# Routed rows of a mixture-of-experts layer scattered to their tokens by job, and read back by four plain loads

## The reference

```python
base_y = _silu_mul_mlp(xt, base_gate_up, base_down)      # 256 -> 2*704 -> 256
top_w, top_e = jax.lax.top_k(rw, 2)                      # of 8 experts
combine = (one_hot(top_e, 8) * top_w[..., None]).sum(1)
moe_y = einsum('eth,te->th', expert_outputs, combine)
return moe_y + base_y
```

## Time and profile before

| | us |
|---|---|
| runs | 904.8, 913.33, 916.46 |
| median of the runs | 913.33 |
| the profiled execution, its own time | 920.24 |
| its span | 918.5 |
| PE busy in the span | 830.7 (90%) |
| DVE busy | 518.9 (56%) |
| ACT busy | 415.4 (45%) |
| POOL busy | 343.8 (37%) |

### The profile page before, as it was taken

The page is one execution under the profiler, slowest core; times in us unless marked ns, Lnnn a source line. Parts: engine busy times, 40 slices in busy tenths (PEclk is TensorE's granted clock), DMA queues, the critical chain, the costliest instruction groups (busy, mean ns, idle before and its releaser), DMA issues.

```text
span 918.5 us, 16141 instructions
## 1 busy us (share of the span) xinstructions
PE 830.7 (90%) x5468; PEld 601.0 (65%) x5469; DVE 518.9 (56%) x1277; ACT 415.4 (45%) x907; POOL 343.8 (37%) x654
## 2 busy tenths in 40 slices
PE   4779799999999999999999896866999999999993
PEld 3344486686776876866866775753566666666672
DVE  3666448768888887888888873564511111111114
ACT  2658756556665656656666362113212222222220
POOL 1146358358367465654672581003330000000005
PEclk9889879779989899799799796896999999999997
DMA  7613242141140141031211211009554100110104
GB/s 187 149 30 86 47 123 56 24 103 25 24 127 13 29 111 22 27 104 25 39 38 25 52 41 29 2 24 376 208 205 164 35 31 26 34 33 24 34 23 132
DMA packets 107618, 66.30 MB, mean 72 GB/s; under 512 B 65120, under 2 KB 98976, under 8 KB 107552
## 3 DMA queue, kind: packets, MB, share of 16 engines
q1 hardware_dynamic: 100160, 59.52, 24.0%
q0 software_dynamic: 1536, 4.20, 1.5%
q10 hardware_dynamic: 5856, 1.73, 0.8%
HBM read 50.84 MB, written 14.58 MB: 71 GB/s over the span
## 4 chain that ended last, share of the span: by engine, by line
PE 67%; ACT 4%; POOL 3%; DVE 3%; DMA 3%; issue 2%; SPq 0%; ACTq 0%; DVEq 0%
PE bank L1693 12%; PE bank L637 8%; PE bank L1772 7%; PE bank L683 5%; PE bank L1710 4%; PE bank L794 3%; PE bank L745 3%; PE bank L760 3%; PE bank L721 2%; PE bank L719 2%; PE bank L759 2%; PE bank L1732 2%; PE bank L645 2%; PE bank L764 2%; PE bank L1763 2%
## 5 line engine op out<-in xcount | busy, mean ns | idle before, releaser
L1133 DVE SCALAR_TENSOR_TENSOR y<-bank,cwh,y 128x510 f32<-128x510 f32 (+2 forms) x240 | 177.1, 743 | 48.5 <-ACT y L887 44.4
L637 PE MATMUL bank<-xnT,wbuf 128*128 128x512 f32 x320 | 159.0, 621 | 6.2 <-DVE y L1133 6.2
L1693 PE MATMUL bank<-f_wgu,f_xgT 128*128 x368 | 118.7, 466 | 0.0
L1441 POOL TENSOR_TENSOR term<-inv,blk 128x126 f32<-128x126 f32 (+22 forms) x248 | 87.4, 352 | 47.1 <-DMA blk<-a_blocks 28.3
L2147 POOL DMA_INDIRECT f_back<-slots_y,f_slot x16 | 15.4, 960 | 222.1 <-DMA slots_y<-f_yb 217.0
L1444 POOL TENSOR_TENSOR inv<-inv,term 128x126 f32<-128x126 f32 (+22 forms) x248 | 91.1, 367 | 19.4
L637 PEld LDWEIGHTS bank<-xnT,wbuf 128*128 128x128 f32 x320 | 56.5, 195 | 63.2 <-issue 50.7
L1693 PEld LDWEIGHTS bank<-f_wgu,f_xgT 128*128 128x128 f32 x368 | 66.3, 190 | 37.2 <-issue 7.7
L2049 DVE TENSOR_TENSOR f_act<-f_sg,bank 128x352 f32<-128x352 f32 x46 | 24.0, 521 | 109.5 <-PE bank L1693 109.5
L1857 ACT ACTIVATE f_sg<-bank 128x352 f32<-128x352 f32 x46 | 21.3, 463 | 123.9 <-PE bank L1693 123.9
L887 ACT ACTIVATE y<-bank,cwh 128x512 f32<-128x512 f32 x80 | 54.9, 686 | 36.1 <-PE bank L637 33.8
(11 more groups left out here) (222 smaller groups left out, 1570.5 us busy)
## 6 DMA issues: line engine op xcount, KB each, us to landing
f_wgu<-in_exp_gu SPq DMA_DIRECT2D x8, 1408.0 KB, 9.3
f_wdn<-in_exp_dn SPq DMA_DIRECT2D x8, 640.0 KB, 10.5
dr<-sums SPq DMA_DIRECT2D x16, 256.0 KB, 4.5
ex<-sums SPq DMA_DIRECT2D x16, 256.0 KB, 4.4
blk<-a_blocks SPq DMA_DIRECT2D x32, 128.0 KB, 2.7
slots_x<-oT SPq DMA_DIRECT2D x24, 128.0 KB, 1.9
f_xg<-slots_x SPq DMA_DIRECT2D x24, 128.0 KB, 2.0
slots_y<-f_yb SPq DMA_DIRECT2D x23, 128.0 KB, 1.7
```

Of the source, the lines that this page charges most:

```text
L637: last = mm(bankA[p % 2][:, :], wbuf[A.par][:, kt, wblk, :], xnT[:, kt, (p % 2) * 512:(p % 2 + 1) * 512], start=kt == 0, stop=kt == 1)
L1133: v.scalar_tensor_tensor(out=y[p % 2][:, :, k:], in0=src[:, :, 0:SEQ - k], scalar=cwh[A.par][:, cb, 3 - k:4 - k], in1=y[p % 2][:, :, k:], ...
L1441: g.tensor_tensor(step_term, inv[:, 0:r, j:j + 1].to_broadcast([P, r, k]), blk[:, j:j + 1, j + 1:].to_broadcast([P, r, k]), ALU.mult).then ...
L1693: last = mm(gu[c][:, 0:FFH], xgT[par][:, k, :], wgu[:, e, k, at:at + FFH], start=k == 0, stop=k == 1)
```

## The change

Two DRAM tensors are new. `rows_back` has a row for each choice and token (2 x 1,024 rows of 1 KB, in the order choice, tile, token) and 256 spare rows. `homes` has one 4-byte number for each of the 3,072 slots: the row of `rows_back` that belongs to the slot.

- DVE makes two small integer tables from new columns of the constant masks (`homes`, behind `place`): `home` (16 columns, the row number of each token and choice) and `spare` (24 columns, a spare row for each slot). The masks grow by 40 columns.
- SP writes `spare` over all of `homes` before it waits for the scatter of the rows. Partition p holds the numbers of slots p, 128 + p, 256 + p and so on, so each is an element of 4 bytes by itself.
- POOL, behind the scatter of the rows, scatters `home` into `homes` by 16 indirect DMAs of 128 numbers, through the same `slot` addresses.
- SP waits for these behind `fetch(3)`, and loads `homes` into the SBUF tile `target` (128 x 24 numbers) by one DMA.
- For each job POOL scatters `yb` straight to its rows of `rows_back` through `target[:, m]`, waits until that has landed, and frees the buffer (`f_free`). The 23 plain stores of SP and `slots_y` are no longer used.
- At the end SP waits for the last two scatters and loads `rows_back` by four plain DMAs of 512 KB into SBUF that held the weights of ways 1 and 2. Each covers four tiles and one choice.
- DVE adds in four batches of four. The four adds of a batch touch different tiles and have no wait between them. `add_base` of tile 6 now stands before all batches, that of tile 7 between the second and the third.

```diff
+    back = wgu[:, 1:3, :, :]... [:, 0:2 * TT_N * HID] ...  # (p, choice j, tile n, d)
@@ sync_program
             if e == WAYS - 3:
                 sp.wait_ge(f_x2t, 8)
+                sp.wait_ge(f_homes, 2)
+                sp.dma_start(homes_of.rearrange("(m p) a -> p (m a)", p=P), spare[:, :], ...).then_inc(f_homes, 16)
                 sp.wait_ge(f_scattered, 32 * TT_N)
...
         fetch(3, 1, 1)
+        sp.wait_ge(homes_out, 16 * 2 * TT_N)
+        sp.dma_start(target[:, :], homes_of.rearrange("(m p) a -> p (m a)", p=P), ...).then_inc(f_homes, 16)
         with sp.Fori(0, JOBS // 2 - 1) as i:
-            store(2 * i, 0)
             fetch(2 * i + 4, 0, i + 2)
-            store(2 * i + 1, 1)
             fetch(2 * i + 5, 1, i + 2)
-        for m in range(JOBS // 2 * 2 - 2, JOBS):
-            store(m, m % 2)
+        sp.wait_ge(y_out[0], 16 * ((JOBS + 1) // 2))
+        sp.wait_ge(y_out[1], 16 * (JOBS // 2))
+        for g in range(2):
+            for j in range(2):
+                n0 = j * TT_N + g * TT_N // 2
+                sp.dma_start(back[:, j, g * TT_N // 2:(g + 1) * TT_N // 2, :],
+                             rows_back[n0 * P:(n0 + TT_N // 2) * P].rearrange("(n p) d -> p n d", p=P)).then_inc(back_in[2 * g + j], 16)
@@ vector_program
-            dve.wait_ge(y_out[par], 16 * use + 1)
+            dve.wait_ge(f_free, m + 1)
             v.tensor_copy(yb[par][:, :], dn[par][:, 0:HID]).then_inc(f_y, 1)
...
+        def add_back(g, j):
+            dve.wait_ge(back_in[2 * g + j], 16)
+            if j:
+                dve.wait_ge(f_back, TT_N * g + 4)
+            for n in range(4 * g, 4 * g + 4):
+                v.scalar_tensor_tensor(out=acc[:, n, :], in0=back[:, j, n, :], scalar=small[:, 2 + j, n:n + 1], in1=acc[:, n, :],
+                                       op0=ALU.mult, op1=ALU.add).then_inc(f_back, 1)
@@ gpsimd_program
-        for k in range(2 * TT_N):
-            if k >= 4:
-                pool.wait_ge(f_back, k - 3)
-            g.indirect_dma_start(out=back[k % 4][:, :], out_offset=None, in_=rows_y,
-                                 in_offset=bass.IndirectOffsetOnAxis(ap=slot[:, k % 2, k // 2:k // 2 + 1], axis=0)).then_inc(back_in[k % 4], 16)
+        pool.wait_ge(f_homes, 2 + 16)
+        for n in range(TT_N):
+            for j in range(2):
+                g.indirect_dma_start(out=homes_of, out_offset=bass.IndirectOffsetOnAxis(ap=slot[:, j, n:n + 1], axis=0),
+                                     in_=home[:, j * TT_N + n:j * TT_N + n + 1], in_offset=None).then_inc(homes_out, 16)
+        pool.sem_inc(f_free, 2)
+        pool.wait_ge(f_homes, 2 + 16 + 16)
+        for m in range(JOBS):
+            pool.wait_ge(f_y, m + 1)
+            g.indirect_dma_start(out=rows_back, out_offset=bass.IndirectOffsetOnAxis(ap=target[:, m:m + 1], axis=0),
+                                 in_=yb[m % 2][:, :], in_offset=None).then_inc(y_out[m % 2], 16)
+            pool.wait_ge(y_out[m % 2], 16 * (m // 2 + 1))
+            pool.sem_inc(f_free, 1)
```

More of the change, by code:

```diff
@@ L62, in mask_table @@
     out["filled"] = np.broadcast_to(P * np.arange(TT_N), (P, TT_N))
+    out["home"] = P * np.arange(2 * TT_N)[None, :] + t
+    out["spare"] = 2 * T + P * (np.arange(SLOT_TILES) % 2)[None, :] + t
     return {k: v.astype(np.float32) for k, v in out.items()}
@@ L1504, in feed_forward @@
     dn = t["banks"][6:8]
+    rows_back = nc.dram_tensor("rows_back", (2 * T + 2 * P, HID), F32, kind="Internal").ap()
+    homes_of = nc.dram_tensor("homes", (SLOT_TILES * P, 1), mybir.dt.uint32, kind="Internal").ap()
     masks, gam, gwT = t["masks"], t["gam"], t["gwT"]
@@ L1534, in feed_forward @@
     yb = [sb(f"f_yb{i}", [P, HID]) for i in range(2)]
-    back = [sb(f"f_back{i}", [P, HID]) for i in range(4)]
+    home = sb("f_home", [P, 2 * TT_N], mybir.dt.uint32)
+    spare = sb("f_spare", [P, SLOT_TILES], mybir.dt.uint32)
+    target = sb("f_target", [P, SLOT_TILES], mybir.dt.uint32)
     x2T = sb("f_x2T", [P, KT_H, T])
@@ L1613, in sync_program @@
                 sp.wait_ge(f_x2t, 8)
+                sp.wait_ge(f_homes, 2)
+                sp.dma_start(homes_of.rearrange("(m p) a -> p (m a)", p=P), spare[:, :], allow_slow_non_contiguous=True).then_inc(f_homes, 16)
                 sp.wait_ge(f_scattered, 32 * TT_N)
@@ L2074, in keep_routed, with homes @@
             dve.sem_inc(f_add, 1)
-        def add_back(k):
-            n, j = k // 2, k % 2
-            dve.wait_ge(back_in[k % 4], 16 * (k // 4 + 1))
-            if some(k):
-                dve.wait_ge(f_back, k)
-            v.scalar_tensor_tensor(out=acc[:, n, :], in0=back[k % 4][:, :], scalar=small[:, 2 + j, n:n + 1], in1=acc[:, n, :],
-                                   op0=ALU.mult, op1=ALU.add).then_inc(f_back, 1)
+        def add_back(g, j):
[5 more added lines that the diff above has]
+                                       op0=ALU.mult, op1=ALU.add).then_inc(f_back, 1)
+        def homes():
+            v.tensor_copy(home[:, :], masks[:, MASK_AT["home"][0]:MASK_AT["home"][0] + 2 * TT_N]).then_inc(f_homes, 1)
+            v.tensor_copy(spare[:, :], masks[:, MASK_AT["spare"][0]:MASK_AT["spare"][0] + SLOT_TILES]).then_inc(f_homes, 1)
         dve.sem_inc(f_act, 2 * LEAD)
@@ L2092, in vector_program @@
         place()
+        homes()
         for b in range(3, FT):
@@ L2115, in vector_program @@
         dve.wait_ge(f_add, JOBS + BASE_FIRST)
[L2116 to L2117 removed]
         add_base(JOBS + BASE_FIRST, BASE_FIRST)
[L2119 to L2120 removed]
+        add_back(0, 0)
+        add_back(0, 1)
         add_base(JOBS + BASE_FIRST + 1, BASE_FIRST + 1)
         dve.wait_ge(f_add, TT_N + JOBS)
[L2123 to L2124 removed]
+        add_back(1, 0)
+        add_back(1, 1)
     def gpsimd_program(pool):
```

23 lines of the change are left out of this document (6 added, 17 removed).

## The result

The changed kernel took 929.8 us (median of 4 runs, 924.37 to 933.01) against 913.4 for the kernel before (4 runs, 904.8 to 916.46): ratio 1.018, 95% interval 1.0137 to 1.0224. The forecast was 905.7, in a range of 897 to 914, so it was wrong. The profiled execution took 924.37 us with a span of 922.6, the fastest of its runs, while the one of before (920.24) was slower than all four of its own. So I compare stretches of the spans, not their totals.

What follows compares the result with a forecast made beforehand. PE was taken to bound the jobs, POOL's gathers the end. The end saves 7.6 us, all else hidden or nothing: profiled 920.24 becomes 912.6, and the same step from the median 913.33 gives 905.7 us, range 897 to 914.

Steps and rivals of the forecast that it cites:

- The end: From the last job's copy to span end: four plain loads replace gathers, DVE's adds bound it; 7.6 us less.
- the step's middle estimate: Four end loads of 512 KB: first lands 3.6 us after issue, at 897.9, the others at 900.1, 902.3 and 904.5.
- the gathers' 22 us: POOL's gathers and transfers at the end hold 22.2 us; PE's base work hidden behind them becomes bare, saving only 7.6.
- Sixteen number scatters on POOL: Before job 0, 676.6 to 696.8, sharing DMA engines with the last weights; 0 to 2.4 us on PE's path, taken as 0.
- Both bounds: Price of a 4-byte number packet: 8.9 ns from 4-byte reads, 46 ns from a 1 KB row of an indirect scatter.
- fetch 2 late, PE waits at the turning for job 2: Before job 2: rows land at 694.7, PE turns them at 697.5, so 2.8 us to spare against number scatters.
- The prediction's own sign of being wrong: In the changed profile: number scatters making the last weights land more than 3 us later would show the forecast wrong.
- dear 4-byte writes: Rival, 677 to 700: number writes delay fetch 2; gain shrinks to 5.2 us or becomes a loss; chance 9%.
- Its law: Same rival's mechanism: at c ns a number packet, fetch 2 is late by 112c - 2.8 us and PE waits.
- the step's upper bound: First write of spare numbers: 1.7 to 8.8 us plus 2.0 to land, in by 660.5 to 667.6; hidden.
- SP's wait for the numbers: Ahead of fetch 4: numbers in by about 698.3, SP at fetch 3 only at 700.55, so no wait.
- Casts, masks, POOL's scatter in the loop, jobs of 8.59 us: Casts 0.4 us, hidden; masks 0.1 us, taken as nothing; POOL's scatter about 3 us of each 8.59 us job, taken as nothing.

Runs made afterwards that it cites:

- e3: Changed kernel without any number traffic through DRAM, job places from a fixed table; median 906.3 us, ratio 0.9897 to the kernel before.
- e2: Changed kernel without the 16 number scatters, first write of spare numbers kept, places from a fixed table; 908.6 us in its one execution.
- v1b: v1 run again, unchanged, on the chip that showed late releases in e4b and e5; median 931.3 us, ratio 1.0196 to the kernel before.
- e1: Changed kernel with the first write of spare numbers in runs of 96 bytes instead of single numbers; median 934.2 us, ratio 1.0211.
- s1: Changed kernel with POOL waiting for the adds of the first six tiles before the number scatters; median 921.2 us, ratio 1.0054.
- e5: Changed kernel without a number table: number and expert ride in each routed row, POOL works out targets per job; median 907.8 us, ratio 0.9916.
- e4: Changed kernel with the numbers 512 bytes apart in DRAM, first execution; 907.6 us, stretch 232.90.
- v1: e3 plus the 16 number scatters in their old place before job 0, with nothing waiting for them; median 933.9 us, ratio 1.0169.
- v5: v1 with each number scatter waiting until the one before has landed; median 931.9 us, ratio 1.0153 to the kernel before.
- s3: e3 plus 16 more scatters of 1 KB rows to a spare tensor where the numbers were; median 910.3 us, ratio 0.9925.
- s3b: s3 run again, unchanged, to stand beside v1b on one chip; median 910.7 us, ratio 0.9953 to the kernel before.
- s4: e3 plus the 16 number scatters, one behind each of jobs 0 to 15; median 905.9 us, ratio 0.9894 to the kernel before.
- s2: Changed kernel with each number scatter waiting until the one before has landed; median 944.5 us, ratio 1.0319 to the kernel before.
- e4b: e4 run again, unchanged, with six more executions; 924.8 to 936.9 us, ratio 1.0214 to the kernel before.
- p64: Changed kernel with the numbers 64 bytes apart in DRAM; 934.2 us in one execution, stretch 258.78.
- p16: Changed kernel with the numbers 16 bytes apart in DRAM; 936.9 us in one execution, stretch 258.93.

## Why the prediction was wrong

- **The end** was right. The step said 7.6 us less, the trace shows 8.1, and e3 about 9 by ratio. The scatter landed after 2.4 us (2.7 taken), the adds took 0.43 us each (0.42 taken), DVE did not wait for a load, and behind the last add lay 2.4 us (2.4 taken). The loads themselves were slower than the step's middle estimate, 4.5 to 7.3 us from issue to landing, and it had time to spare for that. (The Trainium skill, "DMA: Bandwidth & Descriptors", section "Anatomy of one DMA", gives its formula for DMAs on GpSimd's path; the step used it for SP's, and nothing hung on it.) That the gathers' 22 us would mostly be taken up by PE's base work was the point that kept the gain small, and it held.
- **"Sixteen number scatters on POOL ... 0 to 2.4 us on PE's path. I take 0"** is the step that failed. They cost about 25 us: stretch 258.70 against 233.73 without them (e2) and 232.92 without any numbers (e3), or a ratio of 1.018 against 0.9897 (e3), some 3% of 913. Both bounds were prices of the packets themselves, 8.9 and 46 ns. That was the wrong quantity. The number packets do hold only 1.6% of the engines, in v1b and in the changed kernel; the price is paid by weights that travel beside them, at two to 2.7 times the time per packet, and SP, which waits for way 6 before it fetches for job 2, hands it on to the rows. The chain "fetch 2 late, PE waits at the turning for job 2" was named in the step, with 2.8 us to spare; PE waited 14.3 us, and 7.6 more for the rows of jobs 0 and 1, which the step didn't have. The prediction's own sign of being wrong, last weights more than 3 us late, is there too: way 6 and 7's gate and up weights landed 25.9 us after their issue (median of the two), against 8.9 before.
- **The rival "dear 4-byte writes"** had the right place and the right victim and 9%, of which 2% at most for slower by over 2%. Its law (late by 112c - 2.8 us) needs c = 153 ns for a wait of 14.3 us, a number that no row of its own packets shows: they hold 17 ns each (1.6% of 272 us over 254). The first write of the spare numbers landed after 18.0 us, where the step's upper bound was 10.8, and e1 showed that this is worth nothing. The Trainium skill, "DMA: Bandwidth & Descriptors", section "Specifications", says that below 512 bytes a DMA engine reads, modifies and writes. By size alone, 4-byte writes should be alike at any distance. The traces don't bear that out: neighbours slowed the weights (246 to 298 ns a packet) and numbers 16 to 512 bytes apart did not (87 to 105), though all are 4 bytes. Nor does it say that other traffic pays, which is what the 255 ns against 96 show.
- **A mechanism I did not have at all**: the late release. It stood in the trace of before as `remote` in front of DVE's adds, 4.58 and 7.38 us, and I took the stretch of 656 to 679 for bound by PE. Had I asked what a run twice as long would do to it, I would have had a rival worth some 20 us, with a row behind it. It isn't what the changed kernel's own trace shows, which has none; whether its other three executions had any is not known.
- **SP's wait for the numbers: "so no wait"** came out true in the changed kernel, though only since SP was late itself (fetch 3 at 712.89, last number issued 683.91). In s1 it did cost.
- **Casts, masks, POOL's scatter in the loop, jobs of 8.59 us**: as forecast. From 747.17 to 755.76 is one job, and each row scatter landed after 2.4 us.

What stays open: why weights slow down beside neighbouring 4-byte writes, and why only beside ways 6 and 7; what the late release is, and what decides whether an execution has it; and that both roads end at nearly the same stretch (258.70 and 257.96 by the weights, 258.80 by late releases, 258.83 with both). It may be chance, or one cause seen in two forms; v1b's 252.12 speaks for the former, but its execution was the fastest of four. The spread of the kernel before (904 to 921) is larger than the 2 us that its late releases seem to be worth (234.84 against e3's 232.92), so its runs don't tell.

## What to carry to other kernels

Bound the price of a new transfer not only by its own packets but by what they do to the traffic beside them: the same 2,048 numbers cost nothing behind the jobs and 3% of the kernel beside the weights. If small writes have to stand beside large loads, spacing them 16 bytes or more apart kept the loads at full pace here, though it did nothing against late releases. Better still, let small data ride in rows that travel anyway, as e5 does. And when the trace shows an engine released by nothing in sight, ask what grows with the change before calling the stretch bound by something else; and never judge a cure by one execution, nor by times alone: e4 took 907.6 us, then 924.8 to 936.9, and only the traces show that it had removed one of two causes.

## What the runs showed of the hardware

- While POOL issues indirect DMAs back to back, VectorE, ScalarE and SP can be released late by PE's signals, until 2.5 to 5.0 us behind the last of the run: in v1 the first two stood for up to 22.0 and 38.9 us. With waits between the number scatters it was gone from the second on (v5). It comes and goes: one chip showed it in four kernels and, later, in none of two; another in all four. With 16 more scatters of rows instead of numbers (s3, s3b) it was not seen, but neither was it in anything that ran beside them, so whether rows would hold up as much as numbers was not shown.
- 128 numbers of 4 bytes scattered to DRAM land after 3.1 us on quiet queues (s4), and beside weights after 14.6 us side by side and 5.1 us at 512 bytes apart (e4); 128 rows of 1 KB after 2.4 and 6.1 us. 3,072 numbers written singly took 17.5 to 18.2 us beside row scatters (changed kernel, e2, s1, s2) and 6.6 us, 512 bytes apart, in e4; in runs of 96 bytes 1.5 us.
- Runs of such number scatters side by side, beside ways 6 and 7, took SP's loads to 246 to 298 ns a packet (changed kernel, e1, v1, v1b). With the numbers 16, 64 or 512 bytes apart it was 87 to 105 (e4, e4b, p64, p16), without numbers 107 (e3).
